# Scores between the halves of the weighing, subtraction first on VectorE, exchange of the maxima behind the fourth group

## What is computed

```python
B, C, H, W = (4, 256, 64, 64)
CQ = C // 4
xf = x.reshape(size[0], size[1], -1)              # x here is _gn(x)
f = jnp.einsum('qc,bcn->bqn', Wq, xf)
g = jnp.einsum('qc,bcn->bqn', Wk, xf)
h = jnp.einsum('vc,bcn->bvn', Wv, xf)
scores = jnp.einsum('bqn,bqm->bnm', f, g)
beta = jax.nn.softmax(scores, axis=1)
o = jnp.einsum('bvn,bnm->bvm', h, beta)
out = gamma[0] * o + xf                           # and x + out is returned
```

## Time and profile before

| | |
|---|---|
| median of the timed runs | 1973.55 us (3 runs, 1973.13 to 1974.58) |
| the profiled execution | 1974.76 us |
| its span, first to last instruction | 1973.0 us |
| mean granted clock of TensorE, of 2.4 GHz | 0.993 |
| TensorE busy in matmuls | 1899.5 us, 96% |
| VectorE, ScalarE, GpSimd busy | 82%, 81%, 66% |

### The profile page before, as it was taken

The page is one execution under the profiler, slowest core; times in us unless marked ns, Lnnn a source line. Parts: engine busy times, 40 slices in busy tenths (PEclk is TensorE's granted clock), DMA queues, the critical chain, the costliest instruction groups (busy, mean ns, idle before and its releaser), DMA issues. The chain is left out here.

```text
span 1973.0 us, 44069 instructions
## 1 busy us (share of the span) xinstructions
PE 1899.5 (96%) x17476; PEld 1565.3 (79%) x17476; DVE 1617.9 (82%) x1961; ACT 1590.3 (81%) x1699; POOL 1299.8 (66%) x746
## 2 busy tenths in 40 slices
PE   2889999999999999999999999999999999999999
PEld 1578888887788888888777888888878788888887
DVE  7778899888777899897876889998787778878784
ACT  3588888988777888898876888889887688888885
POOL 2066767876546766887554677688655476676776
PEclk9899999999999999999999999999999999999999
DMA  3012212211112121221110221121111011111111
GB/s 110 12 31 73 75 23 54 73 31 23 49 23 69 46 75 30 61 67 23 47 25 17 74 73 54 24 75 53 30 41 32 18 33 33 23 32 31 32 32 35
DMA packets 193629, 86.97 MB, mean 44 GB/s; under 512 B 149137, under 2 KB 186257, under 8 KB 193425
## 3 DMA queue, kind: packets, MB, share of 16 engines
q1 hardware_dynamic: 193424, 84.16, 16.2%
HBM read 46.60 MB, written 16.78 MB: 32 GB/s over the span
## 5 line engine op out<-in xcount | busy, mean ns | idle before, releaser
L310 POOL TENSOR_TENSOR PL<-SC,PH 128x1024 f16<-128x1024 f32 x512 | 1091.3, 2137 | 636.3 <-ACT SC L524 634.3
L416 PE MATMUL O<-V,PH 128*128 128x257 f16 x4096 | 1119.9, 273 | 9.4 <-POOL PL L310 5.2
L418 PE MATMUL O<-V,PL 128*128 128x257 f16 x4096 | 1119.8, 273 | 0.0
L417 PE MATMUL O<-V,PH 128*128 128x256 f16 x4096 | 1118.1, 273 | 0.0
L523 ACT ACTIVATE PH<-SC 128x1024 f16<-128x1024 f32 x512 | 540.6, 1056 | 134.3 <-PE O L418 121.6
L714 DVE TENSOR_TENSOR SC<-SC,MB 128x1024 f32<-128x1024 f32 x512 | 614.9, 1211 | 0.4
L517 ACT ACTIVATE SC<-S 128x1024 f32<-128x1024 f32 x512 | 502.5, 1012 | 124.5 <-issue 106.2
L674 DVE TENSOR_TENSOR XM<-S,XM 128x1024 f32<-128x1024 f32 x384 | 468.1, 1219 | 130.6 <-PE S L404 129.2
L524 ACT ACTIVATE SC<-SC 128x1024 f32<-128x1024 f32 x512 | 534.8, 1044 | 0.0
L416 PEld LDWEIGHTS O<-V,PH 128*128 128x128 f16 x4096 | 406.6, 99 | 59.2 <-DVE OSB L750 6.0
L417 PEld LDWEIGHTS O<-V,PH 128*128 128x128 f16 x4096 | 401.3, 98 | 50.7
(11 more groups left out here) (84 smaller groups left out, 1138.5 us busy)
## 6 DMA issues: line engine op xcount, KB each, us to landing
xin<-x SPq DMA_DIRECT2D x24, 1024.0 KB, 5.9
xres<-x SPq DMA_DIRECT2D x64, 256.0 KB, 2.9
out<-RES SPq DMA_DIRECT2D x64, 256.0 KB, 2.2
ATT<-OT SPq DMA_DIRECT2D x1008, 16.0 KB, 1.9
SC<-x SPq DMA_DIRECT2D x4, 1024.0 KB, 8.7
GG<-GG SPq DMA_DIRECT2D x32, 128.0 KB, 2.4
SC<-wvT SPq DMA_DIRECT2D x1, 256.0 KB, 9.4
SC<-wqT SPq DMA_DIRECT2D x2, 64.0 KB, 10.5
```

Of the source, the lines that this page charges most:

```text
L310: pool.tensor_tensor(PL[:, s % RING, :], sc(s), PH[:, s % RING, :], ALU.subtract).then_inc(pl_ready, 1)
L416: mm(o[:, 0:C + 1], PH[:, n % RING, cols], vh, start=t == 0, stop=False)
L417: mm(o[:, 0:C], PH[:, n % RING, cols], vl, start=False, stop=False)
L418: w = mm(o[:, 0:C + 1], PL[:, n % RING, cols], vh, start=False, stop=t == T - 1)
```

## The change

Three things, in the loops of TensorE and VectorE; no instruction is added or taken away.

1. TensorE: the scores of groups n + 16 and n + 17 stand behind `weigh(n, 0)`, where they stood ahead of it. The waits that belong to them move along.
2. TensorE and VectorE: the exchange of the maxima (`share_maxima`, then `column_maxima` and `spread_maxima`) stands at the very end of group 3, behind `weigh(n, 1)` and behind a projection at the place END; it stood between the halves.
3. VectorE, at even groups: subtract, odd maximum, even maximum, in place of odd maximum, subtract, even maximum.

```diff
@@ tensor
                 b, j = divmod(k, CPB)
-                if g % 2 == 0 and k + 2 < K:
...
-                    scores(n + 2 * G)
                 pe.wait_ge(pl_ready, n + 1)
...
                 weigh(n, 0)
+                if g % 2 == 0 and k + 2 < K:
+                    nb, i = divmod(k + 2, CPB)
+                    if i == 0:
+                        pe.wait_ge(fg_done, nb * NFG + g + 2)
+                    if g == 0 and i % 2 == 0:
+                        pe.wait_ge(g_in[i // 2], 16 * (nb + 1))
+                    if g == 4:
+                        pe.wait_ge(mxc_ready, k + 2)
+                    scores(n + 2 * G)
                 extra(k, g, MID)
+                if g == 0 and k > 0:
+                    pe.wait_ge(osb_ready, MB2 * (k - 1) + 1)
+                weigh(n, 1)
+                extra(k, g, END)
                 if g == 3 and k + 1 < K:
                     read = min(n + 2 * G + 1, K * G)
                     pe.wait_ge(s_stored, read)
                     pe.wait_ge(s_maxed, read)
                     share_maxima(k + 1, S[:, 0, :])
-                if g == 0 and k > 0:
-                    pe.wait_ge(osb_ready, MB2 * (k - 1) + 1)
-                weigh(n, 1)
-                extra(k, g, END)
@@ vector
-                if g % 2 == 0 and k + 2 < K:
-                    maximum(n + 2 * G + 1)
                 if n + SUB_LEAD < K * G:
                     subtract(n + SUB_LEAD)
                 if g % 2 == 0 and k + 2 < K:
+                    maximum(n + 2 * G + 1)
                     maximum(n + 2 * G)
...
+                extra(k, g, MID)
+                extra(k, g, END)
                 if g == 3 and k + 1 < K:
                     column_maxima(k + 1, S[:, 0, :])
                     spread_maxima(k + 1)
-                extra(k, g, MID)
-                extra(k, g, END)
```

More of the change, by code:

```diff
@@ L473, in _ @@
                 b, j = divmod(k, CPB)
-                if g % 2 == 0 and k + 2 < K:
-                    nb, i = divmod(k + 2, CPB)
-                    if i == 0:
-                        pe.wait_ge(fg_done, nb * NFG + g + 2)
-                    if g == 0 and i % 2 == 0:
-                        pe.wait_ge(g_in[i // 2], 16 * (nb + 1))
-                    if g == 4:
-                        pe.wait_ge(mxc_ready, k + 2)
-                    scores(n + 2 * G)
                 pe.wait_ge(pl_ready, n + 1)
```

## The result

| | before | after |
|---|---|---|
| median of the timed runs | 1973.34 us (4 runs, 1971.13 to 1974.58) | 2004.04 us (4 runs, 2003.87 to 2004.74) |
| span of the profiled execution | 1973.0 us | 2003.0 us |
| mean granted clock | 0.993 | 0.991 |

The ratio is 1.0157, with a 95% interval of 1.014 to 1.0175. The change costs some 31 us. The sign was forecast, the size was not: 1985.2 us, with 1992 as the upper end.

A forecast was written before the change was run, and what follows sets the result against it. TensorE, busy 1899.5 of 1973.0 us, was taken as the bound. Per boundary 3.5 - 0.7 + 0.1 + 1.1 + 0.7 = 4.7, three of them 14.1, start 0.7, clock -3.2: +11.6, giving 1985.2 us; range 1978 to 1992.

The forecast's parts named there:

- (d): Rival: some 48 plain chunks each lose 0.1 us at switches between scores and weighing, 1990 us; 0.07 with anything slower.
- the new wait of the scores for the column maximum: Chunk 13: group 4's scores wait 1.4 us for VectorE's column maximum, which stands behind group 3's low parts.
- chunk 13: Boundary chunk with projections: later odd stores delay roundings and projections, then the scores wait; it ends 3.5 us late.
- chunk 14: A half weighing ahead of the exchange shortens its wait from 2.09 to about 1.1 us; -0.7 us without clock.
- chunk 16: Late odd store delays the first value projection's rounding and the next projection, 0.9 us; group 3 adds 0.2; sum 1.1.
- Start: First scores move behind the first half, +1.5 us; the exchange's 0.68 with its 0.16 goes; +0.7 in all.
- I take 0: Low weights in chunks 7 to 11: 2.7 us in hand, 1.2 left after the change, so no cost.
- Any wait for low weights: Sign of being wrong: TensorE in the changed profile waiting anywhere for low weights.
- that wait grows by 0.7 us: Chunk 6: the later exchange delays VectorE's column maximum, so TensorE's 1.03 us wait for output scaling grows by 0.7.
- rival (a): Clock falls at new or grown waits (chunk 6, twice chunk 13, chunk 16), chunk 14's drops stay; 1993 us, chance 0.13.
- a plain chunk cannot become shorter than it is: Plain chunks: TensorE never stops and no matmul is removed, so they stay at 27.4 us.
- the forecast 3.2 us: Clock drops behind chunk 14's wait at two boundaries, 1.6 us each, taken as gone: -3.2 us.

The follow-up runs named there:

- Experiment 9: Changed kernel with the odd maximum ahead of the subtraction again at group 4 of twelve chunks behind the normalisation; 1993.6 us, ratio 1.0099.
- Experiment 6: Changed kernel with the two small coefficient operations on VectorE reading PSUM instead of SBUF; 1989.05 us, ratio 1.0083.
- experiment 10: Kernel before with only the two small coefficient operations reading PSUM instead of SBUF; 1971.04 us, ratio 0.9991.
- Experiment 1: Kernel before with only VectorE's order changed (subtract, odd maximum, even maximum); 1994.4 us, ratio 1.0111.
- experiment 2: Kernel before with only the scores moved between the halves, exchange and VectorE's order as before; 2038.91 us, ratio 1.0338.
- experiment 4: Changed kernel with VectorE's old order at even groups (odd maximum, subtract, even maximum); 1983.34 us, ratio 1.0057.
- experiments 5: Changed kernel with the exchange ahead of the projection at END and the column maximum ahead of the low parts; 2001.88 us, ratio 1.0151.
- experiment 3: Kernel before with only the exchange moved behind the fourth group, column maximum behind the low parts; 2010.52 us, ratio 1.0193.
- the last four experiments: Changed kernel, odd maximum first in twelve places, 1993.6 us; kernel before, PSUM coefficients, 1971.04; changed kernel, both repairs, 1977.02; fastest version, 1959.09.

## Why the prediction was wrong, point by point

2004 us is slower than every rival to which the prediction gave a price; it had 0.07 for (d) and anything slower together.

**Right.** The mechanism at the boundaries: the new wait of the scores for the column maximum (1.32, forecast 1.4), chunk 13 (+3.75, forecast +3.5), chunk 14 (-2.9, forecast -0.7 - 1.6 = -2.3 where the clock had fallen; chunk 46, where it had not, -1.3, forecast -0.7), the exchange's wait of 1.05 with the clock at 1.00 there, chunk 16 (+0.9, forecast +1.1). Start, boundaries and clock together: forecast +9.5 (0.7 + 10.5 - 5.3 + 0.3 + 3.3), measured +8.5.

**Wrong: "I take 0" for the low weights.** This step failed, and cost 10.4 us. It compared the time at which TensorE wants the weights, 1.5 us earlier, with the time at which GpSimd delivered them in the trace of before. It left out that the same change delays the delivery, by another 1.8 us: odd maximum behind a subtraction, odd store behind the odd maximum, exponentials behind the store, GpSimd behind the exponentials. I had followed that very chain in chunk 13, and took it as plain slack everywhere else. The margin of 2.7 us was the smallest that the low weights had, 1.5 of it was spent in my own text, and "if that cover were gone, each such chunk would cost what is missing" was where the work had to start. "Any wait for low weights" stood among my own signs of being wrong. Experiment 9 shows the step by itself.

**Wrong: chunk 6, "that wait grows by 0.7 us".** The forecast had VectorE without a hole from the column maximum to the scaling, and the delay of the column maximum against TensorE came out as said (1.23 - 0.43 = 0.8). But it took the durations behind it as fixed. Two of them last until GpSimd's running instruction ends, so a shift of VectorE against GpSimd changed them, by 1.5 us together; and two maxima in a row take 0.23 more than a maximum and a subtraction. The wait grew by 2.73, not 0.7, and the clock then fell, 2.75 more: that is rival (a) with its mechanism, at one of the four places it named, once in each of the three batches, though at a wait twice as long as it supposed. At its other places the clock stayed. Experiment 6 takes 15.7 us out of these chunks, 3.3 of which experiment 10 takes out of the kernel before too. Between the two kernels of these experiments, both without these two stalls, the chunks 6 differ by 2.7 us in sum where I had forecast 2.1: the other 12.4 of the 15.1 us are the longer stalls and the clock behind them.

**Wrong: "a plain chunk cannot become shorter than it is".** It became 0.12 us shorter, 4.1 in 33 chunks. The sentence took the exchange's 0.22 us for the work of its matmuls, and "it never stops" for granted. The exchange was held by VectorE's last maximum in every plain chunk, 0.05 us ahead of it and 0.08 in it. Experiment 1 shows this with the exchange at its old place.

**Clock.** The three chunks 14 gave 7.3 us back: 3.2 of clock, as forecast, the rest order. The drops in the three chunks 6 took some 6.9 (15.1 less three times 2.73). The length of the wait does not decide. The exchange of the chunks 14 waits 2.09, 2.37 and 2.42 us both in the kernel before and in experiment 2. Before, the granted clock fell behind the first two (0.88, 0.83) and not the third; in experiment 2 it held behind the first (1.00) and fell behind the other two (0.83 each). After 2.00 us it fell in all three batches (experiment 4), after 2.46 in the first alone (experiment 1), after 3.76 in eight of nine cases (changed kernel, experiments 5 and 9). It never fell behind the changed kernel's waits of 1.05 to 1.39, yet it did in experiment 3 behind two waits of 0.77 and 0.85 us, 1.2 us apart. The page cited in the prediction, the Trainium skill's "TensorE: Matmul & The Clock Gate", section "HAM oscillation — how this bites in real kernels", warns of gaps longer than the 2.00 us of experiment 4; where it and the row differ, the row decides. The prediction found no such gap in the loop. There is one ahead of its first weighing, 5.25 us, with a granted clock of 0.77 over the 7.2 us behind it, and the 3.76 us of the changed kernel's chunk 6 is another. What decides beside the length stays open. Runs of the kernel before differ too: of the 21 beside the last four experiments, five took 1971.2 to 1971.6 us at a mean granted clock of 0.995 or 0.996, the others 1973.1 to 1974.6 at 0.992 to 0.994. So it was in part luck that the forecast 3.2 us came out in size: they are the two drops of the one execution that was profiled.

## What to carry to other kernels

When a change moves an engine's demand and the chain that supplies it, work out both for every small margin in the loop, at every kind of stage, before writing a 0; a chain that is computed at one place must be run through at all others where the engines at its ends have extra work. A long duration on a tiny instruction can be a wait in disguise, and no constant: look for whose end it coincides with, and try an operand in another memory. An exchange that starts 0.1 us after what it needs has no margin either, though the profile shows no wait there. And parts of a change can repair each other (67, 39 and 23 us alone, 31 together), so single parts don't price the whole; leaving one part out of the whole tells what it costs there (20.7 us for subtract-first).

## What the runs showed of the hardware

- `tensor_scalar` on 128 x 4 values from SBUF to SBUF took 0.88 to 1.67 us with GpSimd at work, ending within 0.03 us of its running instruction, and 0.17 with GpSimd idle; from PSUM 0.12 to 0.16. The copy L605 of 128 x 2 values, ahead of them, shows the same in both kernels, 1.17 us in the loop and 0.17 in the prologue; no experiment removed it. The normalisation L654, of the kind of L622, took 0.80 or 0.81 us in 12 of its 24 places, where GpSimd ran nothing until its end, and 2.28 to 2.53 in the 12 where GpSimd was already at work.
- Two maxima of 128 x 1024 in a row, the second waiting for the first's result, take 2.49 us to the next instruction, a maximum and an independent subtraction 2.26, two subtractions in a row 2.25 (275.74 to 277.99, before). No run separates the dependence as the cause.
- The exchange's two small float32 matmuls held TensorE for 0.22 us where the maximum that releases them had ended 0.10 us before they started, and for 0.14 where it had ended 0.54 us before or more; the place was the same in the kernel before and in experiment 1.
- The granted clock fell behind some waits of 2.09, 2.42, 2.46 and 3.76 us and held behind others of the same length; the cases stand above under "Clock".
